# Four loads of x from re-laid inputs, and one of the last four output additions split between ScalarE and GpSimd

## The chip, the cores and the metric

The kernel runs on one core of a Trainium2 chip. Its time is device microseconds (us) of one execution. A core has TensorE (matrix products; PE in the rows, with PEld its weight loads), VectorE (DVE), ScalarE (ACT), GpSimd (POOL) and SyncE (SP), which here only issues transfers. Sixteen DMA engines move the data.

## The reference

The input x has 2 batches of 1024 tokens with 256 channels. Four residual stages follow one another, cut here to what is computed:

```
x = x + zX*lap_x(x) + zY*lap_y(x) + zR*x*(1-x)         # stencil: lap_x along the channels, lap_y along the tokens
x = x + softmax(mask(tanh(x@W1+b1)@v)) @ x / count      # pooling over 1024 tokens, mask by the prompt type
x = x + concat(gelu(x@fc1+b)@fc2+b, gelu(...)@We+be)    # one of 16 experts, chosen by index, for 64 of 256 channels
for e in 9 experts (8 routed, 1 shared):
    x = x + gate[e] * ((silu(x@Wg[e]) * (x@Wu[e])) @ Wd[e])      # 256 -> 1024 -> 256
```

## The kernel before, in words

x is held transposed in `xT`: 128 partitions, two chunks of 128 channels (`DC` = 2), 2048 tokens. The tokens are worked on in four blocks of 512 (`TB`). `x_rows`, laid out by the host, has a row for each channel with a reflected row at either end.

The five engines run their own instruction lists, written out by hand, and meet at semaphores. No scheduler orders anything. The stages are:

- **The head (0 to about 39 us).** SP loads batch 0 of x in two halves (`x_load(0, 0)`, 528 tokens, and `x_load(0, 1)`, 496 tokens; line 293), then the small weights, then the fc weights into `raw`, then batch 1 of x and its neighbour rows (`x_up`, `x_nb`). TensorE meanwhile runs seven products on an identity matrix (`keep_warm`, line 1194), and then `neighbours`, products of xT with a fixed matrix `beside` that add up the channels beside each channel. VectorE starts with `stencil_tokens` (lines 696 to 703: `x_nb` from xT) and goes on with squares and sums until `xT` holds the stencil's result (line 744). Scores and softmax of batch 0 follow.
- **The fc stage (about 39 to 155 us)**, products in pairs of high and low parts. The stencil and pooling of batch 1 run in its gaps.
- **The nine experts.** For each expert 16 groups of products are issued, and the results of the down products gather in four banks of PSUM. `outputs_added(e, r, h)` on VectorE (line 1053) multiplies a bank by the expert's gate and adds it to xT, one instruction for each of the two channel chunks. `h` is the token block within the pair `r`.
- **The tail.** After the last group VectorE makes `h_lo` (line 1030), then runs `outputs_added(8, 1, 1)`, whose products end first, and `outputs_added(8, 1, 0)`. `acc_read` counts each of the four additions. SP waits for the count before each of the last stores of 256 KB (line 342), in the same order. The kernel ends when all stores have landed.

GpSimd makes constants in the first 11 us, `v_wide` (line 406) among them, and issues two adding DMAs for batch 1; after 31 us it does nothing. `p5_copy` is a buffer of 128x512 that ScalarE and VectorE use in each group.

Of the kernel before, what the change touches and what calls it, by code (L numbers as in the profile page):

```python
# [5 lines left out]


def stencil_attention_experts(nc, x_rows, scalars, types, expert_ids, w1, b1, v, fc1_w, fc1_b, fc2_w, fc2_b,
                              experts_w, experts_b, moe_w, out):
    f32 = mybir.dt.float32  # L10
    f32r = mybir.dt.float32r
# [1 line left out]
    ALU = mybir.AluOpType  # L13
    ACT = mybir.ActivationFunctionType
    AX = mybir.AxisListType.X

    P = 128
    B, S = x_rows.shape[1:]
    D = x_rows.shape[0] - 2
    DC = D // P  # L20
    T = B * S
    TB = 512
    NT = T // TB
# [5 lines left out]
    E = moe_w.shape[0]  # L29
# [13 lines left out]
    with ExitStack() as ctx:  # L43
        def sb(name, shape, dt=f32):
            return ctx.enter_context(nc.sbuf_tensor(name, shape, dt))

        def sem(name):
            return ctx.enter_context(nc.semaphore(name))


        xT = sb("xT", [P, DC, T])
# [5 lines left out]
        gate = sb("gate", [P, E, NT])  # L57
# [17 lines left out]
        def place(name, offset, shape, dt=f32):  # L75
            return nc.alloc_sbuf_tensor_at(name, shape, dt, offset=start + offset)
# [83 lines left out]
        p5_copy = place("p5_copy", FREE, [P, TB])  # L160
# [3 lines left out]
        ps = ctx.enter_context(nc.psum_tensor("ps", [P, 8, TB], f32))  # L164

        FC_OUT = 2
        ACC = 0
# [16 lines left out]
        x_in = [[sem(f"x_in{b}_{h}") for h in range(NTB)] for b in range(B)]  # L184
# [74 lines left out]
        down0_done = sem("down0_done")  # L259
        down1_done = sem("down1_done")  # L260
        acc_read = sem("acc_read")
        stored = sem("stored")

        ZX, ZY, ZR, SG, GP = 0, B, 2 * B, 3 * B, 4 * B
# [2 lines left out]
        CUTS = [(0, TB + 8), (TB + 8, S)]  # L267
# [6 lines left out]
        ROUNDS = 2  # L274
        GROUPS = ROUNDS * FC
# [4 lines left out]
        def starts(e, i, n):  # L280

            return isinstance(e, int) and e * GROUPS + i < n

        def fc2_cols(tile, b, c):
            at = FC2[b] if c == 0 else FC2B[b]
            return tile[:, at:at + FC * P].rearrange("p (k m) -> p k m", m=P)

        @block.sync
        def _(sp):
            def x_load(b, h):  # L290

                s0, s1 = ((0, CUTS[0][1] + 8), (CUTS[0][1] + 8, S))[h]
                sp.dma_start(xT[:, :, b * S + s0:b * S + s1],
                             x_rows[1:1 + D, b, s0:s1].rearrange("(c p) s -> p c s", p=P)).then_inc(x_in[b][h], 16)

            def neighbours_load():

                sp.dma_start(x_up[:, 1, :, :], x_rows[2:2 + D, 1, :].rearrange("(c p) s -> p c s", p=P)) \
                  .then_inc(rows_in, 16)
                sp.wait_ge(x1_done, NTB)  # L300
                sp.dma_start(x_nb[:, :, 1:S - 1], x_rows[1:1 + D, 1, 0:S - 2].rearrange("(c p) s -> p c s", p=P)) \
                  .then_inc(tokens_in, 16)

            x_load(0, 0)
            x_load(0, 1)
            sp.dma_start(w1_sb[:, :, :], w1.rearrange("(c p) a -> p c a", p=P)).then_inc(w1_in, 16)
            for side in sides:
                sp.dma_start(b1_sb[side, :], b1.unsqueeze(1)).then_inc(w1_in, 16)
                sp.dma_start(v_sb[side, :], v.unsqueeze(1)).then_inc(w1_in, 16)
            sp.dma_start(raw[:, 0:UP].rearrange("p (c f) -> p c f", c=DC), fc1_w).then_inc(fc1_in, 16)  # L310
            sp.dma_start(fc2_cols(raw, 0, 0), fc2_w[:, :, 0:P]).then_inc(fc_in, 16)
            sp.wait_ge(ids_in, 16)
            for b in range(B):
                sp.dma_start(fc2_cols(raw, b, 1)[:, :, 0:SHARED - P], fc2_w[:, :, P:SHARED]).then_inc(fc_in, 16)
                eid = sp.value_load(ids[0:1, b:b + 1], min_val=0, max_val=experts_w.shape[0] - 1)
                sp.dma_start(fc2_cols(raw, b, 1)[:, :, SHARED - P:P],
                             experts_w[ds(eid, 1), :, :, :].rearrange("e p k m -> (e p) k m")).then_inc(fc_in, 16)
                sp.dma_start(out_bias[SHARED - P:P, b, 1:2],
                             experts_b[ds(eid, 1), :].rearrange("e m -> m e")).then_inc(bias_in, 16)
            x_load(1, 0)  # L320
            x_load(1, 1)
            neighbours_load()

            def piece_load(e, k):
                src = moe_w[e, k, :, :] if isinstance(e, int) else \
                    moe_w[ds(e, 1), k, :, :].rearrange("e p w -> (e p) w")
                sp.dma_start(piece[:, k % RAWS, 0:S1, :], src.rearrange("p (t m) -> p t m", m=P)) \
                  .then_inc(piece_in[k % RAWS], 16)

            sp.wait_ge(fc_split, FCW // LOW)  # L330
            for k in range(FC):
                if k >= RAWS:
                    sp.wait_ge(wlo_done, k - RAWS + 1)
                piece_load(0, k)
            with sp.Fori(1, E) as e:
                for k in range(FC):
                    sp.wait_ge(wlo_done, e * FC + k - RAWS + 1)
                    piece_load(e, k)
            for n, (r, h, c) in enumerate((r, h, c) for r in range(ROUNDS) for h in (1, 0) for c in range(DC)):
                t = 2 * r + h  # L340
                sp.wait_ge(acc_read, (E - 1) * ROUNDS * 4 + n + 1)
                sp.dma_start(out.rearrange("(c p) t -> p c t", p=P)[:, c, t * TB:(t + 1) * TB],
                             xT[:, c, t * TB:(t + 1) * TB]).then_inc(stored, 16)
            sp.wait_ge(stored, 16 * NT * DC)

        @block.gpsimd
        def _(pool):
# [53 lines left out]
            for i in range(2):  # L401
# [9 lines left out]
            pool.wait_ge(tokens_in, 16)  # L411
            pool.dma_start(x_nb[:, :, 1:S - 1], x_rows[1:1 + D, 1, 2:S].rearrange("(c p) s -> p c s", p=P),
                           accum_op=ALU.add).then_inc(tokens_summed, 16)

        @block.scalar
        def _(act):
# [133 lines left out]
            for tb in range(NT):  # L550
                for k in range(FC):
                    n = FC * tb + k
# [41 lines left out]
            def hidden0_high(e, i):  # L594
                n = e * GROUPS + i
                act.wait_ge(hidden0_done, n + 1)
                if not starts(e, i, 2):
                    act.wait_ge(down0_done, n - 1)
                nc.scalar.activation(h0_hi[:, i % 2, :], hidden0[:, :], ACT.Copy).then_inc(h0_hi_done, 1)  # L599

            def hidden1_high(e, i):
                n = e * GROUPS + i
                act.wait_ge(hidden1_done, n + 1)
                if not starts(e, i, 1):
                    act.wait_ge(down1_done, n)
                nc.scalar.activation(h1_hi[:, :], hidden1[:, :], ACT.Copy).then_inc(h1_hi_done, 1)  # L606
# [28 lines left out]
            expert(E - 1, False, True)  # L635
            hidden1_high(E - 1, GROUPS - 1)
            hidden0_high(E - 1, GROUPS - 1)

        @block.vector
        def _(dve):  # L640
# [248 lines left out]
            def token_block(p, h, c):  # L889
                return xT[:, c, (2 * p + h) * TB:(2 * p + h + 1) * TB]  # L890
# [104 lines left out]
            for tb in range(NT):  # L995
                b = tb // NTB
                for k in range(FC):
                    n = FC * tb + k
# [10 lines left out]
                for c in range(DC):  # L1009
                    xs = xT[:, c, tb * TB:(tb + 1) * TB]  # L1010
# [16 lines left out]
            def hidden0_low(e, i):  # L1027
                n = e * GROUPS + i
                dve.wait_ge(h0_hi_done, n + 1)
                nc.vector.tensor_tensor(h0_lo[:, i % 2, :], hidden0[:, :], h0_hi[:, i % 2, :].bitcast(f32),  # L1030
                                        ALU.subtract).then_inc(h0_ready, 1)
# [10 lines left out]
                dve.wait_ge(u1_done, n + 1)  # L1042
                nc.vector.tensor_tensor(hidden1[:, :], silu1[:, :], u_sum[:, :], ALU.mult).then_inc(hidden1_done, 1)  # L1043

            def outputs_added(e, r, h):

                done = (down0_done, down1_done)[h]
                dve.wait_ge(done, (e * ROUNDS + r + 1) * FC)
                for c in range(DC):
                    xs = token_block(r, h, c)  # L1050
                    g = gate[:, e, 2 * r + h:2 * r + h + 1] if isinstance(e, int) else \
                        gate[:, ds(e, 1), 2 * r + h:2 * r + h + 1].rearrange("p e t -> p (e t)")
                    nc.vector.scalar_tensor_tensor(xs, ps[:, ACC + DC * h + c, :], g, xs,  # L1053
                                                   ALU.mult, ALU.add).then_inc(acc_read, 1)
# [34 lines left out]
            hidden1_low(E - 1, GROUPS - 1)  # L1089
            hidden0_mul(E - 1, GROUPS - 1)  # L1090
            hidden0_low(E - 1, GROUPS - 1)
            outputs_added(E - 1, 1, 1)
            outputs_added(E - 1, 1, 0)

        @block.tensor
# [349 lines left out]
```

## Time and profile before

| what | value |
|---|---|
| median of 3 runs | 1221.81 us (1221.79 to 1224.42) |
| profiled execution, own time | 1222.2 us |
| its span, first to last instruction | 1220.4 us |
| PE busy | 1211.7 us (99%) |
| DVE busy | 875.8 us (72%) |
| ACT busy | 636.6 us (52%) |
| POOL busy | 13.0 us (1%) |
| DMA | 39.75 MB, mean 33 GB/s |

The span is 1.8 us shorter than the execution's own time. Busy shares are averages over the span. The change touches only the first and the last few microseconds, where the picture is another one, so those stretches have to be read instruction by instruction in the timeline.

### The profile page before, as it was taken

How to read it: one execution, taken by the hardware profiler on the slowest of the kernel's cores; microseconds unless marked ns; L12 is line 12 of the kernel's file. 1: busy time of each engine (PE TensorE's matmuls, PEld its weight loads, DVE VectorE, ACT ScalarE, POOL GpSimd, SP SyncE). 2: the span in 40 equal slices, each digit the busy share in tenths (PEclk: the TensorE clock that was granted, in tenths of full speed). 3: DMA queues.
4: the chain of work that ended last, by engine and by line, in shares of the span. 5: the costliest groups of instructions: out<-in, count | busy, mean ns of one | idle time of the engine just before them, and what ended most of it. 6: DMA issues, size and time to landing. Idle time of an engine off the chain costs nothing.

```text
span 1220.4 us, 16046 instructions
## 1 busy us (share of the span) xinstructions
PE 1211.7 (99%) x5370; PEld 992.0 (81%) x5370; DVE 875.8 (72%) x1488; ACT 636.6 (52%) x1059; POOL 13.0 (1%) x35
## 2 busy tenths in 40 slices
PE   8999999999999999999999999999999999999998
PEld 4778888888888888888888888888888888888886
DVE  8877777776687668766875787578757775777555
ACT  4656654555455445544554455455545554555443
POOL 4000000000000000000000000000000000000000
PEclk9999999999999999999999999999999999999999
DMA  8311010101011001000100011001000100010000
GB/s 232 65 52 52 14 39 1 40 27 39 1 42 32 30 0 52 26 26 0 52 26 26 0 52 30 21 13 52 26 13 13 52 26 13 13 39 1 17 17 35
DMA packets 20702, 39.75 MB, mean 33 GB/s; under 512 B 7234, under 2 KB 8770, under 8 KB 20546
## 3 DMA queue, kind: packets, MB, share of 16 engines
q1 hardware_dynamic: 19248, 37.30, 10.0%
q0 software_dynamic: 544, 2.10, 0.9%
q8 instruction: 13, 0.21, 0.1%
q10 hardware_dynamic: 882, 0.02, 0.0%
q14 instruction: 15, 0.12, 0.0%
HBM read 37.31 MB, written 2.10 MB: 32 GB/s over the span
## 4 chain that ended last, share of the span: by engine, by line
PE 98%; DVE 1%; ACT 0%; issue 0%; POOL 0%; DVEq 0%; POOLq 0%; ACTq 0%
PE ps L1098 98%; PE ps L1124 0%; DVE xT L1053 0%; PE ps L1162 0%; ACT x_up L442 0%; DVE hidden L1043 0%; DVE u_sum L1036 0%; ACT stage L555 0%; DVE h_lo L1030 0%; DVE h_lo L1000 0%; DVE hidden L1024 0%; DVEq L43 0%; ACT h_hi L559 0%; ACT h_hi L606 0%; ACT h_hi L599 0%
## 5 line engine op out<-in xcount | busy, mean ns | idle before, releaser
L1098 PE MATMUL ps<-xc_hi,w_hi 128*128 128x512 f32 x1008 | 392.2, 389 | 0.1
L1098 PE MATMUL ps<-xc_lo,w_hi 128*128 128x512 f32 x1008 | 392.1, 389 | 0.0
L1098 PE MATMUL ps<-xc_hi,w_lo 128*128 128x512 f32 x1008 | 392.1, 389 | 0.0
L592 ACT ACTIVATE silu<-ps 128x512 f32<-128x512 f32 x144 | 86.3, 599 | 326.9 <-PE ps L1098 326.9
L1098 PE MATMUL ps<-h_hi,w_hi 128*128 128x512 f32 x576 | 224.3, 389 | 0.5 <-ACT h_hi L599 0.3
L1098 PE MATMUL ps<-h_hi,w_lo 128*128 128x512 f32 x576 | 224.1, 389 | 0.0
L1098 PE MATMUL ps<-h_lo,w_hi 128*128 128x512 f32 x576 | 223.8, 389 | 0.0
L1098 PEld LDWEIGHTS ps<-xc_hi,w_hi 128*128 128x128 f32 x1008 | 189.3, 188 | 39.8 <-DVE u_sum L1036 0.5
L1098 PEld LDWEIGHTS ps<-xc_lo,w_hi 128*128 128x128 f32 x1008 | 189.3, 188 | 39.2
L1098 PEld LDWEIGHTS ps<-xc_hi,w_lo 128*128 128x128 f32 x1008 | 189.3, 188 | 39.2
L1017 DVE TENSOR_TENSOR h_lo<-hidden,h_hi 128x512 fp32r<-128x512 f32 x144 | 99.7, 692 | 145.4 <-ACT h_hi L606 145.4
L1036 DVE TENSOR_TENSOR u_sum<-ps,p_copy 128x512 f32<-128x512 f32 x144 | 99.0, 688 | 96.1 <-PE ps L1098 96.0
L571 ACT ACTIVATE ps<-ps 128x512 f32<-128x512 f32 x144 | 83.8, 582 | 133.8 <-PE ps L1098 133.8
L992 DVE TENSOR_TENSOR ps<-ps,p_copy 128x512 f32<-128x512 f32 x144 | 100.8, 700 | 41.3 <-PE ps L1098 41.3
L1098 PEld LDWEIGHTS ps<-h_hi,w_hi 128*128 128x128 f32 x576 | 108.1, 188 | 23.8 <-ACT h_hi L599 0.8
L1098 PEld LDWEIGHTS ps<-h_lo,w_hi 128*128 128x128 f32 x576 | 108.1, 188 | 22.4
L1098 PEld LDWEIGHTS ps<-h_hi,w_lo 128*128 128x128 f32 x576 | 108.1, 188 | 22.3
L585 ACT ACTIVATE silu<-ps 128x512 f32<-128x512 f32 x144 | 86.3, 599 | 61.5 <-PE ps L1098 61.3
L1043 DVE TENSOR_TENSOR hidden<-silu,u_sum 128x512 f32<-128x512 f32 x144 | 99.8, 693 | 15.4 <-DVE u_sum L1036 0.5
L1030 DVE TENSOR_TENSOR h_lo<-hidden,h_hi 128x512 fp32r<-128x512 f32 x144 | 98.4, 683 | 0.8 <-ACT h_hi L599 0.7
L1024 DVE TENSOR_TENSOR hidden<-silu,ps 128x512 f32<-128x512 f32 x144 | 98.0, 681 | 0.0
L886 DVE TENSOR_TENSOR w_lo<-piece,w_hi 128x1152 fp32r<-128x1152 f32 x72 | 97.3, 1351 | 0.0
(145 smaller groups left out, 993.2 us busy)
## 6 DMA issues: line engine op xcount, KB each, us to landing
piece<-in_moe_w SPq DMA_DIRECT2D x72, 384.0 KB, 3.1
out_x<-xT SPq DMA_DIRECT2D x8, 256.0 KB, 2.4
xT<-in_x_rows SPq DMA_DIRECT2D x2, 528.0 KB, 5.1
raw<-in_fc_w SPq DMA_DIRECT2D x1, 1024.0 KB, 6.5
x_up<-in_x_rows SPq DMA_DIRECT2D x1, 1024.0 KB, 9.3
x_up<-in_x_rows POOLq DMA_DIRECT2D x1, 1024.0 KB, 8.6
x_nb<-in_x_rows SPq DMA_DIRECT2D x1, 1022.0 KB, 11.5
x_nb<-in_x_rows POOLq DMA_DIRECT2D x1, 1022.0 KB, 11.5
```

The lines of the kernel that those rows point to most:

```text
L571: nc.scalar.activation(ps[:, BANK_B + i % 2, :], ps[:, BANK_A, :], ACT.Copy).then_inc(seeded, 1)
L585: nc.scalar.activation(silu0[:, i % 2, :], ps[:, BANK_A, :], ACT.Silu).then_inc(silu0_done, 1)
L592: nc.scalar.activation(silu1[:, :], ps[:, BANK_E, :], ACT.Silu).then_inc(silu1_done, 1)
L886: nc.vector.tensor_tensor(w_lo[k][:, :, :], piece[:, k % RAWS, A11:RT, :], w_hi[k][:, :, :].bitcast(f32), ALU.subtract).then_inc(wlo_done, 1)
L992: nc.vector.tensor_tensor(ps[:, BANK_E, :], ps[:, BANK_B + i % 2, :], p5_copy[:, :], ALU.add).then_inc(g1_seeded, 1)
L1017: nc.vector.tensor_tensor(h1_lo[:, :], hidden1[:, :], h1_hi[:, :].bitcast(f32), ALU.subtract).then_inc(h1_ready, 1)
L1024: nc.vector.tensor_tensor(hidden0[:, :], silu0[:, i % 2, :], ps[:, BANK_B + i % 2, :], ALU.mult).then_inc(hidden0_done, 1)
L1030: nc.vector.tensor_tensor(h0_lo[:, i % 2, :], hidden0[:, :], h0_hi[:, i % 2, :].bitcast(f32), ALU.subtract).then_inc(h0_ready, 1)
L1036: nc.vector.tensor_tensor(u_sum[:, :], ps[:, BANK_B + i % 2, :], p5_copy[:, :], ALU.add).then_inc(u1_done, 1)
L1043: nc.vector.tensor_tensor(hidden1[:, :], silu1[:, :], u_sum[:, :], ALU.mult).then_inc(hidden1_done, 1)
L1098: return nc.tensor.matmul(out_ap, lhsT, rhs, start=first, stop=last, skip_group_check=shared)
```

## The change

The host makes two more inputs, `x_left` and `x_right`. They hold the same numbers as x, laid out as batch, partition, chunk, token: for each partition the 528 (or 496) tokens of both chunks lie one behind the other, 4,224 (or 3,968) bytes. The four `x_load`s read them in place of `x_rows`. The neighbour rows are still read from `x_rows`.

In the tail, `outputs_added(8, 1, 1)` is called with one chunk only. The addition for chunk 1 goes another way: ScalarE writes gate times the PSUM bank to `p5_copy`, and GpSimd adds `p5_copy` to xT. SP stores that block last and waits for GpSimd's semaphore `last_added`.

```diff
-                s0, s1 = ((0, CUTS[0][1] + 8), (CUTS[0][1] + 8, S))[h]
-                sp.dma_start(xT[:, :, b * S + s0:b * S + s1],
-                             x_rows[1:1 + D, b, s0:s1].rearrange("(c p) s -> p c s", p=P)).then_inc(x_in[b][h], 16)
+                s0, s1 = ((0, x_left.shape[3]), (x_left.shape[3], S))[h]
+                sp.dma_start(xT[:, :, b * S + s0:b * S + s1], (x_left, x_right)[h][b, :, :, :]).then_inc(x_in[b][h], 16)
...
-            for n, (r, h, c) in enumerate((r, h, c) for r in range(ROUNDS) for h in (1, 0) for c in range(DC)):
+            order = [(r, h, c) for r in range(ROUNDS) for h in (1, 0) for c in range(DC)]
+            order.append(order.pop(2 * NT - 3))
+            for n, (r, h, c) in enumerate(order):
                 t = 2 * r + h
-                sp.wait_ge(acc_read, (E - 1) * ROUNDS * 4 + n + 1)
+                if n == len(order) - 1:
+                    sp.wait_ge(last_added, 1)
+                else:
+                    sp.wait_ge(acc_read, (E - 1) * ROUNDS * 4 + n + 1)
...
+            pool.wait_ge(last_scaled, 1)
+            xs = xT[:, DC - 1, (NT - 1) * TB:NT * TB]
+            nc.gpsimd.tensor_tensor(xs, xs, p5_copy[:, :], ALU.add).then_inc(last_added, 1)
...
+            act.wait_ge(down1_done, E * GROUPS)
+            act.wait_ge(acc_read, E * ROUNDS * NT - NT)
+            nc.scalar.activation(p5_copy[:, :], ps[:, ACC + 2 * DC - 1, :], ACT.Copy,
+                                 scale=gate[:, E - 1, NT - 1:NT]).then_inc(last_scaled, 1)
...
-            def outputs_added(e, r, h):
+            def outputs_added(e, r, h, chunks=DC):
...
-                for c in range(DC):
+                for c in range(chunks):
...
-            outputs_added(E - 1, 1, 1)
+            outputs_added(E - 1, 1, 1, DC - 1)
...
+    by_partition = x.reshape(*x.shape[:2], D // P, P).transpose(0, 3, 2, 1)
+    cut = x.shape[1] // 2 + 16
...
+        "x_left": by_partition[..., :cut],
+        "x_right": by_partition[..., cut:],
```

SyncE's list at the end of the program, before the change:

```order
L327 DMA piece<-in_moe_w 128x768
L335 REGISTER_ALU
L335 COMPARE_AND_BRANCH
L342 DMA out_x<-xT 128x512 [waits acc_read] x8
L43 UNCONDITIONAL_BRANCH [waits stored]
```

And with the change:

```order
L328 DMA piece<-in_moe_w 128x768
L336 REGISTER_ALU
L336 COMPARE_AND_BRANCH
L348 DMA out_x<-xT 128x512 [waits acc_read] x7
L348 DMA out_x<-xT 128x512 [waits last_added]
L43 UNCONDITIONAL_BRANCH [waits stored]
```

The eighth store waits for GpSimd and stands behind the one for VectorE's last block.

VectorE's list at its end, before the change (`ps` are the PSUM banks):

```order
L1024 TENSOR_TENSOR hidden_142<-silu_140,ps 128x512 [waits u0_ps,silu0_done]
L1030 TENSOR_TENSOR h_lo<-hidden_142,h_hi 128x512 [waits h0_hi_done]
L1053 SCALAR_TENSOR_TENSOR xT<-ps,gate,xT 128x512 [waits down1_done]
L1053 SCALAR_TENSOR_TENSOR xT<-ps,gate,xT 128x512
L1053 SCALAR_TENSOR_TENSOR xT<-ps,gate,xT 128x512 [waits down0_done]
L1053 SCALAR_TENSOR_TENSOR xT<-ps,gate,xT 128x512
```

And with the change:

```order
L1037 TENSOR_TENSOR hidden_142<-silu_140,ps 128x512 [waits u0_ps,silu0_done]
L1043 TENSOR_TENSOR h_lo<-hidden_142,h_hi 128x512 [waits h0_hi_done]
L1066 SCALAR_TENSOR_TENSOR xT<-ps,gate,xT 128x512 [waits down1_done]
L1066 SCALAR_TENSOR_TENSOR xT<-ps,gate,xT 128x512 [waits down0_done]
L1066 SCALAR_TENSOR_TENSOR xT<-ps,gate,xT 128x512
```

One addition has left the list, and the second of the remaining three is now the one that waits for the last products.

## Rows read from the trace of the kernel before

**Rows 1.** Page, part 4: the chain that ended last, by engine.
```profile
PE 98%; DVE 1%; ACT 0%; issue 0%; POOL 0%; DVEq 0%; POOLq 0%; ACTq 0%
```

**Rows 2.** Timeline, start: start us, duration us, engine, line, output<-input, [idle before].
```profile
1.99 3.36 PE L1098 MATMUL ps<-ident 128*128 128x128 f32 x14 [1.99 <-POOL ident L354]
...
4.92 0.42 PE L1098 MATMUL ps<-ident 128*128 128x128 f32 x1
...
5.25 0.19 DVE L696 TENSOR_SCALAR x_nb<-xT 128x2 f32<-128x2 f32 x1 [0.55 <-DMA xT<-in_x_rows]
...
5.33 0.50 PEld L1098 LDWEIGHTS ps<-xT,beside 128*128 128x128 f32 x2 [0.28 <-issue]
...
6.99 0.17 DVE L699 TENSOR_SCALAR x_nb<-xT 128x2 f32<-128x2 f32 x1 [0.30 <-DMA xT<-in_x_rows]
```

**Rows 3.** Timeline of SP's queue at the start: issues of loads.
```profile
0.73 0.99 SPq L293 DMA_DIRECT2D xT<-in_x_rows  x2
1.76 0.47 SPq L306 DMA_DIRECT2D w_sb<-in_w  x1
...
6.00 0.60 SPq L311 DMA_DIRECT2D raw<-in_fc_w  x1
```

**Rows 4.** Timeline, 19 to 21 us: where the two engines meet.
```profile
19.43 1.10 PE L1098 MATMUL ps<-x_dn,v_wide 64*128 64x512 f32 x2
...
20.57 0.69 DVE L764 TENSOR_TENSOR x_dn<-ps,blend 128x512 f32<-128x512 f32 x1
```

**Rows 5.** DMA traffic in 3.4 to 4.0 us, then 9 to 10 us.
```profile
DMA packets 133, 0.23 MB, mean 378 GB/s; under 512 B 26, under 2 KB 26, under 8 KB 133
...
DMA packets 51, 0.42 MB, mean 418 GB/s; under 512 B 0, under 2 KB 0, under 8 KB 0
```

**Rows 6.** Timeline of the tail, PE, ACT and DVE.
```profile
1213.24 0.63 PE L1098 MATMUL ps<-h_lo,w_hi 128*128 128x512 f32 x2
...
1213.51 0.63 ACT L599 ACTIVATE h_hi<-hidden 128x512 fp32r<-128x512 f32 x1 [1.35 <-DVE hidden L1024]
...
1214.17 0.69 DVE L1030 TENSOR_TENSOR h_lo<-hidden,h_hi 128x512 fp32r<-128x512 f32 x1 [0.70 <-ACT h_hi L599]
...
1214.78 2.72 DVE L1053 SCALAR_TENSOR_TENSOR xT<-ps,gate,xT 128x512 f32<-128x512 f32 x4
...
1215.21 0.61 PE L1098 MATMUL ps<-h_lo,w_hi 128*128 128x512 f32 x2
```

**Rows 7.** The last stores: issues on SP's queue, and issue to landing.
```profile
1215.55 0.33 SPq L342 DMA_DIRECT2D out_x<-xT  x1
...
1216.87 0.99 SPq L342 DMA_DIRECT2D out_x<-xT  x2
...
DMA to landing us min/median/max: 2.4/2.4/2.6
```

**Rows 8.** Windows of the tail: stretch, length, busy by engine, PEclk, DMA share, GB/s.
```profile
1216.20:1216.50 0.30, 0.00 (x0) 0.00 (x0) 0.30 (x1) 0.00 (x0) 0.00 (x0) 1.00 0.37 143
...
1217.00:1218.00 1.00, 0.00 (x0) 0.00 (x0) 0.50 (x1) 0.00 (x0) 0.00 (x0) 1.00 1.02 377
...
1219.00:1219.50 0.50, 0.00 (x0) 0.00 (x0) 0.00 (x0) 0.00 (x0) 0.00 (x0) 0.50 0.40 139
```

**Rows 9.** GpSimd's groups: line, operation, count, busy us, mean ns, idle before.
```profile
L354 POOL TENSOR_SCALAR_AFFINE_SELECT own_chunk<-own_chunk 72x8 f32<-72x8 f32 x3 | 2.3, 762 | 0.3
...
L406 POOL TENSOR_TENSOR v_wide<-ones,v_sb 128x128 f32<-128x128 f32 x1 | 1.4, 1385 | 0.0
```

**Rows 10.** Timeline of DVE and POOL, 9 to 13 us.
```profile
9.59 1.28 DVE L717 SCALAR_TENSOR_TENSOR poly<-ps,sc_in,poly 128x1024 f32<-128x1024 f32 x1
...
10.64 0.19 POOL L403 TENSOR_TENSOR sel<-sel 128x2 f32<-128x2 f32 x1
...
10.91 1.28 DVE L744 SCALAR_TENSOR_TENSOR xT<-x_nb,sc_in,poly 128x1024 f32<-128x1024 f32 x1
11.07 1.39 POOL L406 TENSOR_TENSOR v_wide<-ones,v_sb 128x128 f32<-128x128 f32 x1
```

More of the change, by code:

```diff
@@ L5, with stencil_attention_experts @@
 from contextlib import ExitStack
-def stencil_attention_experts(nc, x_rows, scalars, types, expert_ids, w1, b1, v, fc1_w, fc1_b, fc2_w, fc2_b,
+def stencil_attention_experts(nc, x_rows, x_left, x_right, scalars, types, expert_ids, w1, b1, v, fc1_w, fc1_b, fc2_w, fc2_b,
                               experts_w, experts_b, moe_w, out):
@@ L261, in stencil_attention_experts @@
         acc_read = sem("acc_read")
+        last_scaled = sem("last_scaled")
+        last_added = sem("last_added")
         stored = sem("stored")
```

## The prediction

> **What bounds the kernel now.** I read the page's chain first: 98% of it is TensorE [rows 1], so between the head and the tail nothing that other engines do moves the end, and the change touches nothing there. What is left is when TensorE's unbroken stretch begins and what follows its last product. Both were read in the timeline.
>
> The head. TensorE warms up from 1.99 us with 14 products (seven calls, each in two passes) at an even pace. The last of them begins at 4.92, 2.93 us after the first, so 2.93/13 = 0.225 us apart, and the next product could begin at about 5.14. It begins at 5.33, with 0.28 us of idle weight loading [rows 2]. The first half of x has landed by 5.25: VectorE starts on it after a wait of 0.55 us, and waits 0.30 us more for the second half, at 6.99 [rows 2]. From there both engines work without a wait for data until they meet: TensorE's second score product ends at 19.43 + 1.10 = 20.53 us, VectorE takes it at 20.57 [rows 4]. So both loads are on the path: the first moves TensorE, the second VectorE, and the later of the two counts.
>
> The tail. The last product ends at 1215.21 + 0.61 = 1215.82 us. VectorE runs four additions without a gap from 1214.78 to 1217.50 [rows 6], one every 0.66 us as the issues behind them tell [rows 7], so the third begins at 1216.10. SP issues a store 0.77 us after the start of each addition: at 1215.55, 1216.21, 1216.87 and 1217.53 [rows 7]. The DMA engines are full from about 1216.4 (a share of 0.37 in the 0.30 us before 1216.50) to about 1219.2 (0.40 of the 0.50 us after 1219.00), at 377 GB/s between [rows 8]. That is 2.8 us for four stores of 256 KB, 0.70 us each. So additions and stores go at nearly one pace, and the end is set as much by the transfers as by VectorE.
>
> **The change part by part.**
>
> *The loads of x.* Count and bytes stay. The idea is one run of 4.2 KB for each partition in place of two of 2.1 KB. What the rows show: with packets of 2.1 KB the engines move 378 GB/s, with packets of 8 KB 418 GB/s [rows 5]. From the two (each over 16 engines, at a share of about 1) a packet of 2,112 bytes takes 89 ns and one of 8,192 bytes 313 ns, so 37 ps a byte and some 11 ns fixed. If the packets really doubled, an engine would have 8 fewer in each load: 0.09 us earlier for the first half, 0.18 us for the second. But xT has its chunks 8 KB apart, and the instruction still says 128x2x528. The write side stays in pieces of 2,112 bytes, so I expect little of this.
>
> Against it stands the issue. The two loads of x took 0.99 us, w_sb 0.47 us, each from a rearranged source; a load of raw from a weight tensor laid out by partition, as x_left is, took 0.60 us [rows 3]. If x_left goes like raw, the first half starts 0.13 us later and the second 0.26 us later. The bounds are then -0.18 us (doubled packets, cheap issue) and +0.26 us (costly issue, same packets). TensorE can use at most 5.33 - 5.14 = 0.19 us of an earlier landing. I take +0.1 us: nearer to the row of raw, since it is the like case, minus a part for the reads. After 20.57 us all of it shifts the rest. The second batch's loads are issued at 16 us, and their use is in the fc stage beside TensorE's work; 0.3 us of delay there is covered by it, and if not it would show as a wait of VectorE on a load, of which there is none now.
>
> The Trainium skill (DMA: Bandwidth & Descriptors, Specifications) says that 512 bytes are the least a transfer needs for line rate, which speaks against any gain from longer runs. By that rule the term for the packets is nothing, and the sum would rise by some 0.1 us; the trace, with 378 against 418 GB/s, does not agree fully.
>
> *VectorE's list* loses one addition of 0.66 us, but the second of its three now waits for the last product. It begins at 1215.82 + 0.04 = 1215.86 us, the third at 1216.52. The stores are issued 0.77 us later, at 1216.63 and 1217.29, where the third and fourth were at 1216.87 and 1217.53: 0.24 us earlier. But a second store, at 1216.21, is gone from between.
>
> *ScalarE's scaling* stands behind its last instruction, which ends at 1213.51 + 0.63 = 1214.14; the products it reads ended at 1213.24 + 0.63 = 1213.87 [rows 6]. A copy of this size takes 0.6 us, so GpSimd can start at about 1214.8. Nothing is behind it in either list.
>
> *GpSimd's addition* of 128x512 from two inputs is not in the trace. The nearest rows: 0.19 us for 128x2 [rows 10], 1.39 us for 128x128 (v_wide) [rows 9]. The second ran beside VectorE's line 744, which reads two SBUF inputs and ended at 12.19 us; v_wide ended at 12.46, 0.27 us after it. The first ran at 10.64 us beside line 717, which reads PSUM and one SBUF input [rows 10], and was not held up. A selection of 72x8 took 0.76 us beside two-input work [rows 9]. So GpSimd stands still while VectorE reads twice from SBUF, and the additions of the tail read PSUM and xT: no hold. Bounds: 0.2 us from below, and 4 x 1.39 = 5.6 us from above if v_wide's time was its own. I take 4 x 0.27 = 1.1 us, since its end so soon after line 744 fits waiting. It then ends at about 1216.0 us, well before it is stored.
>
> The Trainium skill (GPSIMD Engine Reference, When to use GPSIMD) keeps elementwise work on VectorE, GpSimd being about 2 times slower with two inputs. By that rule the addition takes 2 x 0.69 = 1.4 us and ends at 1216.2; the sum stays, since its store waits for its turn anyway.
>
> *SP's last store* stands behind the one of 1217.29 and follows it by one issue of 0.33 us: 1217.62 to 1217.65, against 1217.53 now. This is +0.1 us by the issue. By the transfers it is more. Bytes begin about 0.83 us after an issue (1216.38 - 1215.55). The first store's are through at 1217.08, the second's begin at 1216.63 + 0.83 = 1217.46, and three of 0.70 us end at 1219.56, where before they ended at 1219.2. So a gap of 0.38 us opens in the DMA engines, as the block that could fill it, GpSimd's, is stored last. The tail is +0.35 us by the transfers, +0.1 by the issues; I take +0.3.
>
> *Sum.* Head +0.1, tail +0.3: +0.4 us. Against the profiled execution (span 1220.4, own time 1222.2) that gives 1220.8 and 1222.6. The median of the runs is 0.4 us under the profiled one, so 1221.81 + 0.4 = 1222.2 us.
>
> **The rivals.**
>
> *GpSimd becomes the tail.* Its addition is the last thing before the last store. It decides as soon as it takes over 1217.6 - 1214.8 = 2.8 us. At 5.6 us it ends at 1220.4, the store lands 2.4 us later [rows 7], and the span ends at 1222.8: +2.4 us, 1224.3. If VectorE's additions hold it besides until 1217.2, it ends at 1222.8 and the store at 1225.2: +4.8 us, 1226.7, slower by 0.4%. For it: 1.39 us for only 128 elements. Against it: the small operations beside line 717 and the 0.27 us. A chance of 0.15, of which 0.04 for the far end.
>
> *Both ends gain.* The longer runs bring TensorE its 0.19 us, VectorE 0.18 us, and the tail gains the 0.24 us by which VectorE ends earlier, if the last two stores share the engines without a loss. That is -0.4 us, 1221.4. For it: 378 against 418 GB/s. Against it: DMA engines that are already full in the tail [rows 8]. Chance 0.2.
>
> *The loads don't change.* Packets and issues are as before, the head is even and only the tail counts: +0.3 us, 1222.1. For it: the same shape in the instruction. Against it: the two kinds of issue, 0.47 and 0.60 us. Chance 0.2.
>
> **How the numbers follow.** My forecast has 0.45, the others 0.15, 0.2 and 0.2. All but the far end of the first rival lie within 2.5 us of now. A change of under 0.3% (3.7 us) can't be told from none here, as the three runs alone are 2.6 us apart. Faster by over 0.3% has no mechanism at all; I leave 0.02 for the unforeseen. Slower has 0.04 from the far end and 0.02 besides. Same: 0.92. The range of the terms is -0.18 - 0.24 below and +0.26 + 0.35 above, so 1221.4 to 1222.4; I widen it to 1221.0 and, for the nearer end of the first rival and a median drawn from the upper of such runs, to 1224.3.
>
> **What would show it.** In the head: the start of VectorE's first work on x and of the first product with `beside`, against 5.25 and 5.33 us, the issues of the two loads against 0.99 us together, and whether packets above 4 KB appear. Where VectorE meets TensorE, 20.57 plus the shift. In the tail: GpSimd's addition with its length, and its end before 1217.6; VectorE's last addition ending at about 1217.2; the last issue at 1217.6; a dip in the DMA share near 1217.2. I am wrong if the fc stage starts other than within 0.3 us of before, if the addition takes over 2.8 us, or if the time moves by over 3.7 us: then something outside both ends, such as the pace of TensorE's products, has changed.

## The result: slower, and the profile after

The changed kernel takes 1226.45 us (median of 22 runs, 1223.06 to 1228.20), the kernel before 1222.03 us (22 runs). The ratio is 1.0032 with a 95% interval of 1.0026 to 1.0038: a loss of some 3.9 us by the ratio and 4.4 by the medians, where I had forecast 0.4. The profiled execution has a span of 1224.5 us, 4.1 more than before.

The executions don't spread evenly. Of the 22, four have a span of 1221.1 us and a mean granted clock of 1.000; ten have 1224.3 to 1224.6 at 0.997 or 0.998; five have 1226.0 to 1226.2 at 0.996 or 0.997; of the other three, two have 1223.5 and one 1225.3. Those of before lie within 3 us of each other. That a program with fixed work comes out in groups, and in step with TensorE's clock, is the first hint at where the time went.

The start of the changed kernel in the timeline (columns as in [rows 2]):

```profile
0.73 0.68 SPq L295 DMA_DIRECT2D xT<-in_x_left  x1
...
6.08 0.18 DVE L709 TENSOR_SCALAR x_nb<-xT 128x2 f32<-128x2 f32 x1 [1.83 <-DMA xT<-in_x_left]
...
6.20 9.01 PE L1111 MATMUL ps<-xT,beside 128*128 128x512 f32 x16 [0.85 <-DMA xT<-in_x_left]
...
11.89 1.28 DVE L730 SCALAR_TENSOR_TENSOR poly<-ps,sc_in,poly 128x1024 f32<-128x1024 f32 x1 [1.66 <-PE ps L1111]
...
15.13 1.93 PE L1111 MATMUL ps<-xT,w_sb 128*64 128x512 f32 x4
...
23.54 3.58 PE L1137 MATMUL ps<-ident,xT 128*128 128x128 f32 x16
...
28.75 3.62 PE L1111 MATMUL ps<-x_up,exp_out 128*8 128x256 f32 x16
```

The same places of the kernel before, as far as [rows 2] doesn't have them:

```profile
5.36 7.55 PE L1098 MATMUL ps<-xT,beside 128*128 128x512 f32 x16
...
6.31 0.19 PEld L1098 LDWEIGHTS ps<-xT,beside 128*128 128x128 f32 x1 [0.48 <-issue]
...
12.84 1.93 PE L1098 MATMUL ps<-xT,w_sb 128*64 128x512 f32 x4
...
21.25 1.96 PE L1124 MATMUL ps<-ident,xT 128*128 128x128 f32 x16
...
24.88 3.62 PE L1098 MATMUL ps<-x_up,exp_out 128*8 128x256 f32 x16
```

Read the two side by side, each start less the start before. VectorE's first work on x is 0.83 us late (6.08 against 5.25), the first product with `beside` 0.84. At the products with `w_sb` it is 2.29 us, so the 16 products between took 1.45 us more. It stays 2.29 up to the transposes (line 1137 here, 1124 before), and is 3.87 behind them, at the products of `x_up`: another 1.6 us. And VectorE, which waited for nothing here before, now waits 1.66 us for TensorE at line 730.

Both steps are TensorE's pace. Its weight loads in the changed kernel:

```profile
8.03 0.34 PEld L1111 LDWEIGHTS ps<-xT,beside 128*128 128x128 f32 x1 [0.52 <-issue]
...
10.32 0.19 PEld L1111 LDWEIGHTS ps<-xT,beside 128*128 128x128 f32 x1 [0.24 <-issue]
```

At 8.03 us a load takes 0.34 us and the next one follows 0.86 later (8.89); from 10.32 on it is 0.19 and 0.43. The step between loads is twice as long at first (0.86 against 0.43 us), so I read it as the lower of the clock's two levels, 1.2 GHz, to about 10 us and 2.4 GHz from there. Before, 0.19 us was reached at 6.31. The granted clock in the windows is 1.00 all through this stretch and doesn't show it; the reading rests on the durations. The granted clock shows a fall that came later (the PEclk column is the third from the end; 23 to 24, 24 to 25 and 28 to 30 us):

```profile
23.00:24.00 1.00, 1.00 (x9) 0.99 (x9) 0.97 (x2) 0.00 (x0) 0.00 (x0) 0.84 1.02 356
24.00:25.00 1.00, 1.00 (x7) 1.00 (x6) 0.97 (x3) 0.00 (x0) 0.51 (x1) 0.50 0.98 307
...
28.00:30.00 2.00, 1.61 (x8) 0.84 (x9) 1.07 (x3) 2.00 (x5) 0.67 (x1) 1.00 0.95 188
```

At 0.50 the engine is at its lower level, 1.2 GHz, and the transposes take 3.58 us in place of 1.96. Before, every window from 5 to 40 us has 1.00. The same products stand ahead of the transposes in both kernels (eight with an output of one column, at 22.67 and at 20.37 us), so why the clock fell in one and not in the other isn't shown.

Why x is late is a matter of the first reads. DMA traffic from 3.00 to 3.25 us, before (above) and after (below; the last two columns are the busy share and GB/s):

```profile
3.00:3.25 0.25, 0.25 (x3) 0.25 (x3) 0.00 (x0) 0.25 (x1) 0.25 (x2) 1.00 0.77 294
```

```profile
3.00:3.25 0.25, 0.25 (x3) 0.25 (x3) 0.00 (x0) 0.25 (x1) 0.25 (x2) 1.00 0.97 117
```

The engines move two fifths as much here, at no lower a share. Two more kernels with these loads, e1 and e3 below, have 70 and 53 GB/s in the same stretch at shares of 0.78 and 0.50, so the low rate is steady and the high share is not. By 3.75 us the rate is the old one. The number of packets in the whole run is 20702 in both kernels, with the same split by size, so the packets did not double to 4.2 KB.

The tail (answers to [rows 6], [rows 7] and [rows 8]):

```profile
1217.77 0.67 ACT L649 ACTIVATE p_copy<-ps,gate 128x512 f32<-128x512 f32 x1
...
1218.51 0.75 DVE L1066 SCALAR_TENSOR_TENSOR xT<-ps,gate,xT 128x512 f32<-128x512 f32 x1
1218.53 1.28 POOL L422 TENSOR_TENSOR xT<-xT,p_copy 128x512 f32<-128x512 f32 x1 [1189.86 <-ACT p_copy L649]
...
1219.61 1.41 DVE L1066 SCALAR_TENSOR_TENSOR xT<-ps,gate,xT 128x512 f32<-128x512 f32 x2 [0.36 <-PE ps L1111]
...
1221.05 0.83 SPq L348 DMA_DIRECT2D out_x<-xT  x2
```

```profile
1220.20:1220.60 0.40, 0.00 (x0) 0.00 (x0) 0.40 (x2) 0.00 (x0) 0.00 (x0) 1.00 1.04 394
...
1220.90:1221.30 0.40, 0.00 (x0) 0.00 (x0) 0.12 (x1) 0.00 (x0) 0.00 (x0) 1.00 0.15 56
...
1221.60:1222.60 1.00, 0.00 (x0) 0.00 (x0) 0.00 (x0) 0.00 (x0) 0.00 (x0) 0.58 1.03 379
```

(`p_copy` is `p5_copy`; the views leave buffer numbers out.) GpSimd's addition takes 1.28 us and ends at 1219.81, long before its store. The hole in the DMA traffic is there, at 1220.9 to 1221.3. From the first addition to the end it is 1224.5 - 1218.51 = 5.99 us; before, 1220.4 - 1214.78 = 5.62 us. In the profile the tail costs 0.37 us.

### The profile page after: what moved, and what is told of

It reads as the page before. It is cut to its first block, busy times and chain, and to the rows that moved or that the text cites. A ratio compares the mean times of both kernels' runs of the same rounds, so it can differ in the third digit from the quotient of the medians.

```text
span 1224.5 us, 16048 instructions
## 1 busy us (share of the span) xinstructions
PE 1214.5 (99%) x5370; PEld 994.2 (81%) x5370; DVE 874.9 (71%) x1487; ACT 637.0 (52%) x1060; POOL 13.4 (1%) x36
## 2 busy tenths in 40 slices
DMA packets 20702, 39.75 MB, mean 32 GB/s; under 512 B 7234, under 2 KB 8770, under 8 KB 20546
## 4 chain that ended last, share of the span: by engine, by line
PE 98%; DMA 0%; ACT 0%; DVE 0%; issue 0%; DVEq 0%; ACTq 0%
PE ps L1111 98%; PE ps L1137 0%; DMA xT<-in_x_left 0%; ACT x_up L451 0%; PE ps L1175 0%; DVE xT L1066 0%; ACT ctx_parts L468 0%; DVE hidden L1056 0%; DVE u_sum L1049 0%; ACT stage L564 0%; DVE hidden L1037 0%; DVE h_lo L1013 0%; DVEq L43 0%; ACT h_hi L568 0%; ACT h_hi L608 0%
```

## The experiments

**The two halves alone.** The changed kernel without its tail, and without its loads:

```diff
 # e1: loads only
-            outputs_added(E - 1, 1, 1, DC - 1)
+            outputs_added(E - 1, 1, 1)             # and no scaling, no GpSimd addition, stores in the old order
 # e2: tail only
-                sp.dma_start(xT[:, :, b * S + s0:b * S + s1], (x_left, x_right)[h][b, :, :, :])
+                sp.dma_start(xT[:, :, b * S + s0:b * S + s1],
+                             x_rows[1:1 + D, b, s0:s1].rearrange("(c p) s -> p c s", p=P))
```

> The four loads from x_left and x_right alone; the tail as before. Clock theory: the first half of x lands some 0.8 us later, TensorE stands idle for 0.85 us after its warm-up, and the products with beside start at the slow clock; the head carries the loss. Expected: 1226.1 us, that is the changed kernel's 1226.45 less the 0.35 us of the tail, and runs in several levels (about 1222.7 to 1227.8). Rival, the tail carries it (GpSimd's addition or its wait): 1222.1 us.

> The split addition and the moved store alone; the loads as before. Clock theory: only the 0.35 us of the store gap, 1222.4 us, and the runs as close together as those of before. Rival, the tail carries the loss: 1226 us.

Loads only: 1225.41 us, ratio 1.0022 (1.0014 to 1.0031). Its executions lie at 1222.5, 1225.0, 1225.9 and 1227.5: the groups of the changed kernel (1223.1, 1225.5, 1226.4, 1228.1) less 0.5 or so. Tail only: 1222.72 us, ratio 1.0004 (0.9995 to 1.0012), all within 1.1 us. The head carries the loss. By its interval the tail alone can't be told from no change; its profile has 1220.7 - 1214.75 = 5.95 us from the first addition to the end, against 5.62 before, so a tail of 0.3 to 0.4 us rests on the two profiles.

The profiled execution of loads only happened to be one of the lowest group (span 1220.7):

```profile
6.12 7.11 PE L1100 MATMUL ps<-xT,beside 128*128 128x512 f32 x16 [0.77 <-DMA xT<-in_x_left]
13.15 1.93 PE L1100 MATMUL ps<-xT,w_sb 128*64 128x512 f32 x4
```

x is as late, and TensorE idle for 0.77 us, but the 16 products run at full pace from the first, in 7.11 us. Before they took 7.55, as the engine's rise fell among them (its first two loads took 0.50 us, those from 6.31 on 0.19). So the 0.31 us by which this kernel reaches `w_sb` after the kernel before is a wait of 0.76 less 0.44 of faster work, and the span is 0.3 us longer. To price late data by itself it has to be set against a kernel with x on time and the same pace. The one that reads only batch 1 from a copy (e10 below) has it:

```profile
5.36 7.11 PE L1098 MATMUL ps<-xT,beside 128*128 128x512 f32 x16
...
12.40 1.93 PE L1098 MATMUL ps<-xT,w_sb 128*64 128x512 f32 x4
```

Its `w_sb` products begin 0.75 us earlier (12.40 against 13.15), its products with `x_up` 0.51 (24.69 against 25.20), and its span is 1220.3 us. So late data by itself costs some 0.4 us of span, by one execution of each. The rest is TensorE's pace.

**More and less warm-up.** The changed kernel with ten calls in place of seven, and the kernel before with four:

```diff
-    WARM = [7, 3]
+    WARM = [10, 3]        # e3, in the changed kernel
+    WARM = [4, 3]         # e5, in the kernel before
```

> The changed kernel with ten warm-up calls on the identity in place of seven, so that TensorE is busy until about 6.2 us, when the first half of x lands. Clock theory: no idle gap, the engine reaches 2.4 GHz before or with the first product with beside; the second fall near 24 us does not come either. Left are the later landing (+0.8 us) and the tail (+0.35): 1223.2 us. Rival, the lateness of the data alone makes the loss, through VectorE's chain: no change, 1226.4 us or more.

> The kernel before with four warm-up calls in place of seven; loads and tail untouched. TensorE is then idle from about 4.1 to 5.3 us, with the data as early as ever. Clock theory: the idle gap alone makes the loss, in levels like those of the changed kernel, 1224 to 1227 us in most runs. Rival, only the landing of the data counts: 1222.0 us, runs close together.

Ten calls: 1224.24 us, ratio 1.0018 (1.0009 to 1.0027), so about half of the loss is gone (the ratio was 1.0032). None of its eleven runs is above 1225.7, where 16 of the changed kernel's 22 lie above 1226. But I had expected 1223.2, and five of the eleven still lie at 1225.5. Four calls in the kernel before: 1224.91 us, ratio 1.0022 (1.0012 to 1.0033), groups from 1223.1 to 1228.2. The second is the cleanest test, since its data came at 5.33 us, as good as on time. TensorE's products in it, where the view ends within the `w_sb` group:

```profile
5.44 10.15 PE L1098 MATMUL ps<-xT,beside 128*128 128x512 f32 x16 [1.37 <-DMA xT<-in_x_rows]
15.52 1.50 PE L1098 MATMUL ps<-xT,w_sb 128*64 128x512 f32 x3
```

and in the one with ten calls, cut off in the same way:

```profile
6.42 7.26 PE L1111 MATMUL ps<-xT,beside 128*128 128x512 f32 x16
13.60 1.07 PE L1111 MATMUL ps<-xT,w_sb 128*64 128x512 f32 x2
```

With TensorE idle for 1.37 us, and loads and tail as before, the 16 products are 2.6 us longer (10.15 against 7.55): late data isn't needed for the loss. The gap and the shorter warm-up came together here, so this run doesn't tell which of the two counts. Without a gap they take 7.26 us though the data is late; but so they do in e1 with a gap, so for ten calls the spread of the runs says more than the one profile.

**The issue of the loads.** The host's rows padded by 16 numbers each:

```diff
+        return np.concatenate([flat, flat[..., :16]], axis=-1)
...
-        "x_left": by_partition[..., :cut],
+        "x_left": padded(by_partition[..., :cut]),
```

> The changed kernel, but the host's rows of x_left and x_right are 16 numbers longer than what is loaded, so that the source can't be read as one unbroken block of 256 rows and keeps its partition, chunk and token dimensions. Issue theory: SP's issue goes back to 0.47 us or less and the first half lands at about 5.25 us as before; then only the tail is left, 1222.4 us. Rival, it is where the new inputs lie in memory or their layout that makes the landing late: 1226.4 us and issues of 0.6 us.

1227.07 us, ratio 1.0031 (1.0021 to 1.0040). The issues went back to 0.46 and 0.47 us, and x landed later still, at 6.92 us. So a short issue does not bring x back in time, and my theory of the issue falls. What the longer issue costs by itself isn't shown, as the padding also changed the spacing of the rows.

**Where the reads go.** Three kernels with the old tail read x from other inputs: from a second copy of x_rows (e8); from `x_left` and `x_right` with each partition's row filled up to 8,192 bytes (e9); and from the copy for batch 1 alone (e10). Then the lists of inputs were reordered:

```diff
 # e8, second copy: "x_copy" handed over behind "x_rows"; e10: for batch 1 only; e13: handed over ahead of it
-                             x_rows[1:1 + D, b, s0:s1].rearrange("(c p) s -> p c s", p=P))
+                             x_copy[1:1 + D, b, s0:s1].rearrange("(c p) s -> p c s", p=P))
 # e9, pitch: each partition's row of x_left and x_right filled up to 2048 numbers; e15: both ahead of x_rows
+        return np.concatenate([flat, flat, flat], axis=-1)[..., :2048]
 # e11, e14: the changed and the padded kernel with x_left and x_right ahead of x_rows
 # e12: the kernel before, x_rows moved from the first place of the list to the last
```

> The kernel before, its four loads of x read from a second input that holds the same rows in the same layout as x_rows. Layout theory: as it is the layout that slows the first microsecond of the reads, nothing changes: landing at 5.25 us, 1222.0 us. Rival, any further input (its place in memory, or its first use) makes the reads slow: landing at 6 us, 1224 to 1228 us.

> The kernel before, its four loads read from rows laid out by partition as in the change, but each partition's row padded to 8,192 bytes, the distance between rows in x_rows. Theory that closely packed rows are read slowly at first: landing at 5.25 us as before, 1222.0 us. Rival, reading both chunks from one place is slow whatever the distance: landing at 6 us or later, 1224 to 1228 us.

> As the second-copy kernel, but batch 0 is read from x_rows and only batch 1, issued at 16 us, from the copy. Theory that it counts from which input the first reads are: landing at 5.25 us and 1222.1 us as before. Rival, that a further input exists is enough: landing at 6 us or later, 1224 to 1228 us.

> The changed kernel with x_left and x_right handed over ahead of x_rows. Theory that the place in the list of inputs counts: the first half lands at 5.3 us or a little earlier, and only the tail's 0.35 us and the longer issue (0.2 us) are left, 1222.6 us. Rival, the place does not count: landing at 6.1 us, 1226.4 us.

> The kernel before with x_rows handed over last, behind the expert weights; nothing else differs. Theory that the place in the list of inputs counts: landing at 6 us or later, 1224 to 1228 us. Rival, only a kernel with a further input is slow: landing at 5.25 us, 1222.1 us.

> As the second-copy kernel, but the copy stands first in the list of inputs and x_rows second. Place theory: landing at 5.25 us, 1222.1 us. Rival, any input but the one that the neighbour rows are read from too is slow: landing at 6.5 us, 1226.4 us.

> The padded version of the changed kernel (issues of 0.47 us) with x_left and x_right first in the list. Theory that place and issue together make the whole delay: landing at 5.3 us, 1222.6 us with the tail. Rival, closely packed rows are slow by themselves: landing at 6 us or later, 1224 to 1227 us.

> The version with rows 8,192 bytes apart, x_left and x_right first in the list, the old tail. Theory that place and issue make the whole delay: landing at 5.3 us, 1222.1 us. Rival, two chunks read from one row are slow: landing at 6 us or later, 1224 to 1227 us.

"Landed" is the start of VectorE's first work on x in the profiled execution; "late group" counts the runs above 1224 us.

| loads of batch 0 from | place | spacing of the rows | landed, us | median, us | ratio (95%) | late group |
|---|---|---|---|---|---|---|
| x_rows, batch 1 from copy (e10) | first | 8,192 B | 5.25 | 1222.20 | 1.0002 (0.9993 to 1.0012) | 0 of 10 |
| copy (e13) | first | 8,192 B | 5.20 | 1222.31 | 1.0000 (0.9990 to 1.0010) | 0 of 10 |
| by partition (e15) | first | 8,192 B | 5.12 | 1222.36 | 1.0002 (0.9993 to 1.0012) | 0 of 10 |
| x_rows (e12) | last | 8,192 B | 6.03 | 1222.68 | 1.0016 (1.0005 to 1.0027) | 4 of 10 |
| copy (e8) | second | 8,192 B | 6.55 | 1226.44 | 1.0036 (1.0023 to 1.0050) | 5 of 5 |
| by partition (e9) | second, third | 8,192 B | 6.92 | 1225.82 | 1.0032 (1.0020 to 1.0045) | 6 of 6 |
| by partition (e11) | first | 4,224 B | 6.16 | 1226.47 | 1.0034 (1.0023 to 1.0045) | 7 of 8 |
| by partition (e14) | first | 4,288 B | 6.85 | 1227.32 | 1.0035 (1.0023 to 1.0048) | 5 of 6 |
| by partition (e4) | second, third | 4,288 B | 6.92 | 1227.07 | 1.0031 (1.0021 to 1.0040) | 9 of 9 |
| by partition (the changed kernel) | second, third | 4,224 B | 6.08 | 1226.45 | 1.0032 (1.0026 to 1.0038) | 18 of 22 |

The last four have the changed tail, the others the old one. The border of 1224 us is rough: the lowest runs of e4 and e14 (1224.01 and 1223.97) have a mean clock of 0.999 and may be late only by their data and tail.

Two of the rows that make the case, of the copy handed over second, and of the same copy handed over first:

```profile
6.55 0.17 DVE L696 TENSOR_SCALAR x_nb<-xT 128x2 f32<-128x2 f32 x1 [1.09 <-DMA xT<-in_x_copy]
```

```profile
5.20 0.23 DVE L696 TENSOR_SCALAR x_nb<-xT 128x2 f32<-128x2 f32 x1 [0.50 <-DMA xT<-in_x_copy]
```

The two programs read the same bytes in the same pattern and differ in the order of two inputs. So the place of the input counts, against what I had expected of e8. But the first place isn't enough: closely packed rows land late there too (e11, e14, both against my expectation), and rows 8,192 bytes apart land in time (e15). Nor is the spacing enough: e9 missed its forecast by 1.67 us. The change failed on both counts: its inputs stood second and third, and they were closely packed. In these kernels x landed in time only with the first place and the wide spacing together. The wide spacing also spreads the reads over more memory, which no run separates from it. What the order of inputs does (where they come to lie in memory, or something that the first transfers find ready) isn't seen in a trace and stays open, as does why packed rows are slow for a microsecond and not after.

The profiles of all these kernels also tell the two steps apart. Where TensorE had no gap ahead of the `beside` products (before, e2, e3, e6, e10, e13, e15), the 16 products take 7.11 to 7.62 us and the 16 transposes 1.96 or 1.97. Where it had one:

| profile of | gap, us | 16 products, us | 16 transposes, us | span, us |
|---|---|---|---|---|
| e1 | 0.77 | 7.11 | 1.97 | 1220.7 |
| e12 | 0.80 | 7.11 | 1.97 | 1220.7 |
| e5 | 1.37 | 10.15 | 1.97 | 1223.0 |
| e9 | 1.68 | 8.59 | 1.97 | 1223.0 |
| the changed kernel | 0.85 | 9.01 | 3.58 | 1224.5 |
| e11 | 0.92 | 8.88 | 3.62 | 1224.5 |
| e8 | 1.32 | 9.27 | 3.33 | 1224.6 |
| e14 | 1.62 | 9.15 | 3.44 | 1225.4 |
| e4 | 1.69 | 9.37 | 3.23 | 1225.4 |

With one execution of each it can't be a rate, but it gives the lower groups of runs a content: neither step, the first alone, or both. The length of the gap doesn't order them.

**The store order in the tail.** The old loads, the split addition, and its block stored second as before:

```diff
-            order.append(order.pop(2 * NT - 3))
...
-                if n == len(order) - 1:
+                if n == 2 * NT - 3:
                     sp.wait_ge(last_added, 1)
```

> The loads as before; the split addition kept, but its block is stored second, in the old order, as GpSimd ends at about 1216.1 us. Theory of the store gap: the second store goes out at about 1216.2 us again, the DMA engines stay full, the third and fourth leave 0.24 us earlier but can't be moved sooner: 1222.0 us, the same as before, 0.35 us under the moved store (1222.7 us measured). Rival, the split itself costs: 1222.4 us or more.

1222.51 us, ratio 1.0003 (0.9994 to 1.0012). By the medians it is 0.2 us under the moved store, but the two were timed on different chips beside different runs of before, and the intervals overlap: they can't tell it from no change either way. The profile says more. The last issue begins 1.77 us after the first (1215.70 to 1217.47), 0.21 us sooner than before (1215.55 to 1217.53), yet from the first addition to the end it is 1220.5 - 1214.93 = 5.57 us, against 5.62 before and 5.95 or 5.99 with the moved store. So the hole is closed, and the earlier issues have bought next to nothing. No version beat the kernel before.

## Why the prediction was wrong

- **The chain and the meeting of the two engines** were read rightly: the shift at 23.54 us is the shift at 15.13, and nearly all of that at 28.75 us (3.87) reaches the first addition of the tail (1218.51 - 1214.78 = 3.73).
- **The step that failed is "TensorE can use at most 0.19 us of an earlier landing ... After 20.57 us all of it shifts the rest."** It priced a later landing at its own length and put TensorE's pace at what it was. The trace of before had the sign: the warm-up products are 0.225 us apart [rows 2], where the transposes of the same size take 1.96/16 = 0.12 us each at 21.25 us; in the changed kernel, at a granted clock of 0.50, they take 3.58/16 = 0.22. So TensorE was still at 1.2 GHz in the warm-up. A gap there is not only its length but also what the engine may do next at half pace: 1.45 us on the `beside` products and 1.6 us on the transposes in the profiled execution. Late data alone costs 0.4 us (e1 against e10). That the first step comes from what TensorE did ahead of x, and not from late data, is shown by e5; what brings the second, the fall near 24 us, stays open. The Trainium skill (TensorE: Matmul & The Clock Gate, Part 1) says that the clock follows how busy the engine has been, and that the moment of change differs between executions since the window is free-running. The groups of runs fit this, and e1 and e12 beside the changed kernel (gaps of 0.77 and 0.80 us without a slow stretch, 0.85 with one); that the window is free-running is not shown by any run here. I had not weighed it, and it would have made a rival with several microseconds.
- **The size of the delay.** I gave the loads -0.18 to +0.26 us, and x landed 0.83 us late. The issue did grow (0.68 us where two took 0.99), as I took from the load of `raw`, but with issues of 0.46 and 0.47 us x landed still later (e4), so it wasn't what held x up. The bounds came from full-rate windows at 3.4 to 4.0 and 9 to 10 us [rows 5]; nothing in them speaks of the first microsecond of another tensor.
- **"The instruction still says 128x2x528"**: right, the packets did not change.
- **The batch 1 loads** cost nothing: right (e10).
- **GpSimd's addition**: 1.28 us, where I took 1.1. That v_wide's 1.39 us was mostly waiting for VectorE is shown: in the changed kernel, where VectorE idles from 10.24 to 11.89 us, v_wide takes 0.40 us (`11.12 0.40 POOL L412 TENSOR_TENSOR v_wide<-ones,v_sb 128x128`). The rival that made GpSimd the tail was rightly held low.
- **The tail**: +0.35 us by the transfers, taken as 0.3; measured 0.37 in the profile, with the hole where it was forecast (0.38 us).
- **The sum** was +0.4 and came out at +3.9. In the profiled execution it is +4.1: the wait for x 0.84, the `beside` products 1.45, the transposes 1.58, less 0.14 that is made up again before the tail, and the tail 0.37. The two terms of pace, 3.0 us, stood nowhere in the sum. The range ended at 1224.3 us and missed (that bound has a slip of 0.1: 1221.81 + 2.4 is 1224.2).
- **The sign of being wrong** was named: that the fc stage starts more than 0.3 us off, and then the pace of TensorE's products. It starts 3.77 us later (38.46 against 34.69). But the prediction looked for it outside the two ends, and it lay inside the head.

## What to carry to other kernels

Look at TensorE's pace, not only at its idle time, wherever it has not yet risen to 2.4 GHz or stands just behind a warm-up: here a wait of 0.85 us there was followed by 3 us of lost pace in one execution and by none in another with 0.80, and it showed as groups among the runs. When a load ahead of such a place is touched, time it by its landing in a trace, since equal bytes in equal packets landed up to 1.8 us apart here. And before a change to the last stores, add up their transfer time: here the DMA engines were full, so issues 0.21 us sooner bought 0.05 us, and storing the earliest block last opened a hole of some 0.4 us.

## What the hardware showed that I had not expected

- The order of the inputs alone moved the landing of the first transfer by 1.35 us (5.20 against 6.55 us), and of x_rows by 0.78 us (5.25 against 6.03).
- Rows 4,224 or 4,288 bytes apart were read late from the first place (6.16 and 6.85 us), rows 8,192 bytes apart in time (5.12 us). From 3.00 to 3.25 us the three kernels with the changed loads in second place moved 53 to 117 GB/s, the kernel before 294.
- ScalarE's small load of the scalars is held up in some of these kernels too: VectorE's first use of it came at 3.90 us before and at 5.55 us in the padded kernel. In the changed kernel it came at 3.49 us, earlier than before, though x was late.
- A gap of about 0.8 us ahead of the `beside` products went without any loss of pace in two profiles (e1, e12) and with it in one (0.85 us).
- Filling the gap with more warm-up does not bring back the lowest time in all runs: five of eleven stayed at 1225.5 us. What makes TensorE rise late there stays open; a profile of such a run was not taken.
